# The fp4 layer of a perceiver kernel: the down product in three one-pass products, with GpSimd taking lower parts and the quantiser's last step

## The reference, cut to what matters

```
def fp4_quant_dequant(x):              # blocks of 16 along the last dimension
    scale = max(max(abs(block)) / 6, 1e-12)
    q = GRID[searchsorted(MID, abs(block / scale))] * sign(block) * scale
def fp4_linear(x, w):  return einsum('bsk,nk->bsn', fp4(x), fp4(w))
x = x + fp4_linear(silu(fp4_linear(ln(x), w_gate)) * fp4_linear(ln(x), w_up), w_down)   # 512 -> 1408 -> 512
```

## Time and profile before

| | |
|---|---|
| median of three runs | 1468.76 us |
| the profiled execution | 1466.26 us, span 1464.4 us, mean TensorE clock 0.981 |
| busy share of the span | TensorE 93%, VectorE 74%, ScalarE 40%, GpSimd 10% |
| the fp4 layer | from about 804 to 1057 us of the span |
| 1 MB loads of the next stage's keys | 7.0 us from issue to landing (page, part 6) |

### The profile page before, as it was taken

The page is one execution under the profiler, slowest core; times in us unless marked ns, Lnnn a source line. Parts: engine busy times, 40 slices in busy tenths (PEclk is TensorE's granted clock), DMA queues, the critical chain, the costliest instruction groups (busy, mean ns, idle before and its releaser), DMA issues. The chain is left out here.

```text
span 1464.4 us, 32483 instructions
## 1 busy us (share of the span) xinstructions
PE 1364.0 (93%) x13794; PEld 940.7 (64%) x13794; DVE 1083.9 (74%) x2221; ACT 587.7 (40%) x1234; POOL 149.3 (10%) x106
## 2 busy tenths in 40 slices
PE   9999999999999997999988889999799898888898
PEld 5677777777777775435565767667466555677443
DVE  5477777778778787773677699787577786765887
ACT  2344444444444433212223511111388885034543
POOL 3200000000000000230000000100000003154800
PEclk9999999999999999899989999999999999989999
DMA  7343344334443333400006000000355464000000
GB/s 263 105 138 100 119 126 130 113 120 142 152 162 125 113 93 119 149 1 1 3 3 240 28 1 1 0 1 1 119 203 229 178 208 158 35 3 2 8 23 29
DMA packets 50330, 136.88 MB, mean 93 GB/s; under 512 B 10974, under 2 KB 15838, under 8 KB 44043
## 3 DMA queue, kind: packets, MB, share of 16 engines
q1 hardware_dynamic: 50186, 134.82, 27.2%
HBM read 117.73 MB, written 17.07 MB: 92 GB/s over the span
## 5 line engine op out<-in xcount | busy, mean ns | idle before, releaser
L735 ACT ACTIVATE l0x_prob<-l0x_prob,l0x_negmax 128x512 f32<-128x512 f32 x128 | 90.9, 712 | 177.5 <-DVE l0x_negmax L802 177.5
L593 PE MATMUL bank<-l0x_ctxT,l0x_upper_k 128*128 128x512 f32 x256 | 106.8, 417 | 1.3 <-PEq L271 1.3
L606 PE MATMUL bank<-l0x_upper_v,l0x_ctxT 128*128 128x512 f32 x256 | 104.7, 409 | 0.0
L608 PE MATMUL bank<-l0x_upper_v,l0x_ctxT_lower 128*128 128x512 f32 x256 | 101.0, 394 | 0.0
L595 PE MATMUL bank<-l0x_ctxT,l0x_lower_k 128*128 128x512 f32 x256 | 100.8, 394 | 0.0
L607 PE MATMUL bank<-l0x_lower_v,l0x_ctxT 128*128 128x512 f32 x256 | 100.7, 393 | 0.0
L594 PE MATMUL bank<-l0x_ctxT_lower,l0x_upper_k 128*128 128x512 f32 x256 | 100.5, 392 | 0.0
L1071 PE MATMUL bank<-ident,l1x_prob 128*128 128x128 f32 x512 | 78.9, 288 | 13.2 <-ACT l1x_prob L1141 9.2
L1141 ACT ACTIVATE l1x_prob<-l1x_prob,l1x_negmax 128x512 f32<-128x512 f32 x128 | 91.0, 715 | 0.0
L1190 DVE CUSTOM_DVE_ANT_0 l1x_prob<-bank,l1x_zeros 128x512 f32<-128x512 f32 x128 | 80.8, 687 | 13.8 <-PE bank L1056 13.8
L1071 PEld LDWEIGHTS bank<-ident,l1x_prob 128*128 128x128 f32 x512 | 55.6, 143 | 51.0 <-ACT l1x_prob L1141 41.2
(11 more groups left out here) (346 smaller groups left out, 3125.6 us busy)
## 6 DMA issues: line engine op xcount, KB each, us to landing
l0x_whole<-in_turned_context SPq DMA_DIRECT2D x16, 1024.0 KB, 5.4
l1x_KT<-in_turned_context SPq DMA_DIRECT2D x16, 1024.0 KB, 7.0
l1x_ctx<-in_ctx SPq DMA_DIRECT2D x16, 1024.0 KB, 4.8
fp_weight<-l0x_weight_piece SPq DMA_DIRECT2D x24, 352.0 KB, 4.8
f_raw<-fp_weight SPq DMA_DIRECT2D x3, 2816.0 KB, 18.6
l0x_abs_piece<-in_L_ffn_w_gate SPq DMA_DIRECT2D x16, 512.0 KB, 4.4
l0x_abs_piece<-in_L_ffn_w_up SPq DMA_DIRECT2D x16, 512.0 KB, 5.4
l0x_abs_piece<-in_L_ffn_w_down SPq DMA_DIRECT2D x16, 512.0 KB, 4.5
```

Source lines behind the costliest of these rows:

```text
L593: nc.tensor.matmul(bank[:, :], w.upper_k[:, kc, cols], c, start=kc == 0, stop=False)
L606: nc.tensor.matmul(bank[:, :], c, w.upper_v[:, kc, :], start=kc == 0, stop=False)
L608: last = nc.tensor.matmul(bank[:, :], c_lower, w.upper_v[:, kc, :], start=False, stop=kc == CH - 1)
L735: nc.scalar.activation(w.prob[r][:, :], w.prob[r][:, :], ACT.Exp, scale=-1.0, bias=w.negmax[:, p:p + 1], accum_out=w.rowsum[:, b % 2, p:p ...
```

## The change

The down product is made of three one-pass products too. Upper parts of the down weights and of the turned hidden values are ScalarE copies; the lower parts, and those of the tokens, are GpSimd subtractions, from whole copies in SBUF. GpSimd also does step 9 of the quantiser for the hidden pieces (`hq_done`); VectorE does steps 0 to 8 (`HQ` = 9) and, since the scratch is shared, waits ahead of step 4 until GpSimd has read it. There are three sets of scale tensors. The first keys load moves to the layer's end. The head's normalised rows go to `w.head`, as `XN` now holds upper down weights; other addresses of the next stage's buffers move.

```diff
 @block.sync
-            loads(sp)
             sp.wait_ge(gate_up_full, TILES * R)
             late_loads(sp)                       # now keys 0, context 0, keys 1, context 1
 @block.gpsimd
+            def lower_tokens(t):
+                pool.wait_ge(x_upper, t + 1)
+                nc.gpsimd.tensor_tensor(w.x_lower[t % 2][:, :, :], w.x_whole[t % 2][:, :, :], w.x_upper[t % 2][:, :, :].bitcast(F32),
+                                        ALU.subtract).then_inc(x_lower, 1)
+            def last_step(t, r):
+                at, n = N0[r]
+                pool.wait_ge(step, (t * R + r + 1) * HQ)
+                if r == 0 and t > 0:
+                    pool.wait_ge(turn_full, t * R)
+                quantisers[(t * R + r) % 2].last(nc.gpsimd, w.hq[:, at:at + n], n).then_inc(hq_done, 1)
+            def lower_down(k):                   # DOWN_PARTS = ((0, 4), (4, 8), (8, IC0))
+                pool.wait_ge(down_upper, k + 1)
+                nc.gpsimd.tensor_tensor(w.down_lower[:, lo:hi, :], w.downT[:, lo:hi, :], down_part(lo, hi).bitcast(F32),
+                                        ALU.subtract).then_inc(down_lower, 1)
+            def lower_hidden(t):
+                for r, (at, n) in enumerate(N0):
+                    pool.wait_ge(h_upper, t * R + r + 1)
+                    nc.gpsimd.tensor_tensor(w.h_lower[:, at:at + n], w.hT[:, at:at + n], hidden_part(at, n).bitcast(F32),
+                                            ALU.subtract).then_inc(h_lower, 1)
+            lower_tokens(0)
+            lower_tokens(1)
+            pool.wait_ge(rstd_done, 1)
+            next_tokens(2)
+            for r in range(R):
+                last_step(0, r)
+                lower_down(r)
+            for t in range(LAST):
+                last_step(t + 1, 0)
+                lower_hidden(t)
+                if t + 2 < TILES:
+                    lower_tokens(t + 2)
+                last_step(t + 1, 1)
+                if t + 3 < TILES:
+                    next_tokens(t + 3)
+                last_step(t + 1, 2)
+            lower_hidden(LAST)
 @block.tensor, turn_hidden(t) and out_product(t)
-                pe.wait_ge(step, (t + 1) * (R * Q_STEPS))
+                pe.wait_ge(hq_done, (t + 1) * R)
-                for kc in range(IC0):
-                    ins = nc.tensor.matmul(work[1][:, :], w.hT[:, kc * P:(kc + 1) * P], w.downT[:, kc, :],
+            def upper_products(bank, lo, hi):
+                for kc in range(lo, hi):
+                    nc.tensor.matmul(bank[:, :], hidden_chunk(kc), down_chunk(kc), start=kc == 0, stop=False)
+                    nc.tensor.matmul(bank[:, :], hidden_chunk(kc), w.down_lower[:, kc, :], start=False, stop=False)
+            def out_product(t):
+                if t == 0:
+                    pe.wait_ge(down_lower, len(DOWN_PARTS))
+                pe.wait_ge(h_upper, t * R + R)
+                upper_products(work[1], 0, IC0)
+                pe.wait_ge(h_lower, t * R + R)
+                lower_products(work[1], 0, IC0).then_inc(out_full, 1)      # 11 of h_lower x down_chunk
 last_tile: per piece wait hq_done, transposes, wait h_upper, upper_products; then wait h_lower, lower_products
 @block.scalar, upper_tokens(t); upper_hidden(t, r) after the three hidden_copy(t, r); upper_down(k) after silu(0, r)
-                nc.scalar.activation(w.x_upper[t % 2][:, :, :], work[0][:, :]..., ACT.Copy).then_inc(x_upper, 1)
+                nc.scalar.activation(w.x_whole[t % 2][:, :, :], work[0][:, :]..., ACT.Copy).then_inc(x_whole, 1)
+                act.wait_ge(x_whole, t + 1)
+                nc.scalar.activation(w.x_upper[t % 2][:, :, :], w.x_whole[t % 2][:, :, :], ACT.Copy).then_inc(x_upper, 1)
 @block.vector, hidden(t); lower_tokens(t) is gone; tokens(t) keeps ten steps and waits for hq_done ahead of step 4
-                    for q in range(Q_STEPS):
+                    for q in range(HQ):
+                        if piece + q > 0:
+                            dve.wait_ge(step, piece * HQ + q)
+                        if q == 4 and piece > 0:
+                            dve.wait_ge(hq_done, piece)
```

More of the change, by code:

```diff
@@ L153, in __call__, with last @@
             return v.scalar_tensor_tensor(xn, pow2, -HALF_STEP, xn, ALU.mult, ALU.add)
-        return v.tensor_tensor(blocks(out), blocks(xn), wide(scale), ALU.mult)
+        return self.last(v, out, n)
+    def last(self, engine, out, n):
+        k, t = n // BLOCK, self.tmp
+        blocks = lambda ap: ap.rearrange("p (k e) -> p k e", e=BLOCK)
+        return engine.tensor_tensor(blocks(out), blocks(t.xn[:, 0:n]), t.scale[:, 0:k].unsqueeze(2).to_broadcast([P, k, BLOCK]),
+                                    ALU.mult)
 Q_STEPS = 10
@@ L2013, with fp4_layer @@
 HEAD_TILES = TILES - 1
-def fp4_layer(nc, g, w, loads, late_loads):
+def fp4_layer(nc, g, w, late_loads):
     s = lambda n: g.sems.take(f"ffn0_{n}")
@@ L2181, in last_tile @@
                     ins.then_inc(turn_full, 1)
[L2182 to L2186, removed]
+                    pe.wait_ge(h_upper, LAST * R + r + 1)
+                    upper_products(LAST_OUT, at // P, (at + n) // P)
+                pe.wait_ge(h_lower, LAST * R + R)
+                lower_products(LAST_OUT, 0, IC0).then_inc(out_full, 1)
                 pe.wait_ge(x_done, LAST)
@@ L2236, in silu, with hidden_copy, upper_hidden @@
                 nc.scalar.activation(w.silu[:, at:at + n], gate[r][:, 0:n], ACT.Silu).then_inc(silu_done, 1)
[L2238 to L2245, removed]
+            def hidden_copy(t, r):
+                at, n = N0[r]
+                act.wait_ge(turn_full, t * R + r + 1)
+                if r == 0 and t > 0:
+                    act.wait_ge(out_full, t)
+                bank = gate[r] if t == LAST else work[r % 2]
+                nc.scalar.activation(w.hT[:, at:at + n], bank[:, 0:n], ACT.Copy).then_inc(turned, 1)
+            def upper_hidden(t, r):
+                at, n = N0[r]
+                act.wait_ge(turned, t * R + r + 1)
+                nc.scalar.activation(hidden_part(at, n), w.hT[:, at:at + n], ACT.Copy).then_inc(h_upper, 1)
             upper_tokens(0)
@@ L2262, in _ @@
                 silu(0, r)
+            for k in range(len(DOWN_PARTS)):
+                upper_down(k)
             for t in range(LAST):
@@ L2369, in _ @@
             tokens(1)
-            lower_tokens(1)
             hidden(0)
@@ L3197, in fp4_buffers @@
         w.downT = a.over("f0_downT", wide, F32, "tm_kT")
+        w.down_lower = a.over("f0_down_lower", wide, F32R, "tm_kT")
+        w.down_upper = [a.over("f0_down_upper0", [P, TILES, D], F32R, "XN"),
+                        a.over("f0_down_upper1", [P, IC0 - TILES, D], F32R, "tm_XX", DOWN_REST_AT)]
+        w.h_upper = [a.over("f0_h_upper0", [P, 8 * P], F32R, "tm_XX", HIDDEN_UPPER_AT),
+                     a.over("f0_h_upper1", [P, INTER0 - 8 * P], F32R, "tm_XX", HIDDEN_REST_AT)]
+        w.h_lower = a.over("f0_h_lower", [P, INTER0], F32R, "tm_kT", size + 3 * INTER0 * 4)
+        w.head = a.over("f0_head", [P, HEAD_TILES, D], F32, "tm_mixed0", 2 * CH * TOK * 4 - size)
         w.silu, w.h, w.hq, w.hT = (a.over(f"f0_{n}", [P, INTER0], F32, "tm_kT", size + i * INTER0 * 4)
```

109 lines of the change are left out of this document (61 added, 48 removed).

## The result

The changed kernel took 1477.01 us (median of five runs, 1474.23 to 1478.64) beside 1467.66 us for the kernel before on the same chip: ratio 1.0065, 95% interval 1.0052 to 1.0078. A second set gave 1475.44 us beside 1467.77, ratio 1.0048 (1.0031 to 1.0064). It is slower, as forecast (1474.0, range 1464 to 1481). One of the nine executions of the experiment "wait by piece" took 2608 us at a granted clock of 0.941; its ratio leaves that one out, and without it the median is 1471.7.

What follows compares the result with a forecast made beforehand. TensorE was taken to bound each steady tile, with VectorE late in the first. Startup +11.0, steady tiles -5.3 and last tile -0.4 sum to +5.3 us: 1471.6 for the profiled execution, median 1474.0, range 1464 to 1481.

Steps and rivals of the forecast that it cites:

- The mechanism of the first tile: First tile: VectorE and GpSimd instructions with two SBUF inputs each wait for the other's whole instruction; startup +11.0 us.
- the walk: First tile followed step by step through the engines: first down product ends at 883.4 against 874.1, 9.3 us later.
- the clock term: First tile: after three TensorE idles of 4 us or more, products run longer at a lower clock; 1.7 us.
- Steady tiles: Tiles between startup and the last: down product 9.4 to 7.55 us, net 0.9 us saved each, six tiles 5.3 us.
- The wait term: Steady tile: down product waits for ScalarE's upper copies, ready 1.0 us after TensorE has turned the tokens.
- the sixth steady tile: Six tiles were counted as one kind, each saving 0.9 us, together 5.3 us.
- The last tile: Tile of 13.4 us: three added waits of 0.6, 0.6, 0.45 and a shorter down product; -0.4 us (0 to -0.6).
- The overlap that I granted: Last tile: waits overlapping the transposes bring its 13.2 us to between 12.8 and 13.2.
- that rival: Steady tile: GpSimd's lower parts come late by more than the 1 us margin; +11 and 1480 us; chance 0.08.
- the 2 to 4 forecast: Steady tile: VectorE gains waits for GpSimd of at most 2 to 4 us, staying under 26.6.
- VectorE as the bound: Every tile: VectorE stopped by GpSimd's two-input work, 29.7 against 27.5 us; total about 1493; chance 0.06.
- Partly stopped: First tile: engines stop each other part of the time, startup +3 to +8, sum -2.9 to +2.9; chance 0.21.

Runs made afterwards that it cites:

- wait by piece: Against the changed kernel, the down product's upper products wait for the upper copies of the hidden values piece by piece; 1472.54 us, ratio to before 1.0021.
- GpSimd alone: Against the changed kernel, the down product is float32 as before, while GpSimd keeps the last steps and token lower parts; 1467.91 us, ratio to before 0.9999.
- split down: Against the changed kernel, GpSimd's down-weight subtractions are eleven 512 wide instead of three 2048 or 1536 wide; 1478.39 us, ratio to before 1.0070.
- down from bank: Against the changed kernel, ScalarE takes the down weights' upper parts and VectorE their lower parts straight from the banks; 1475.30 us, ratio to before 1.0039.
- loads and places: The kernel before with only the later first keys load and the next stage's new addresses; 1470.61 us, then 1467.57 us in a second set.

## Why the prediction was right, and where it was not

**The mechanism of the first tile held.** Forecast for the walk: transposes 862.9, tokens 870.0, lower parts 880.9, end 883.4. Measured: 864.2, 871.5, 881.2, 883.9. The first product ends 10.2 us later from the layer's start than before (10.4 in the second profiles), and tile 1's transposes start 10.0 us later; the forecast was +11.0. Three things in it were wrong. I put the end of the old product at 874.1, while the gate product behind it starts at 873.7, so the walk's 9.3 us should have been 9.7. The stopped steps were 1 and 3, tensor_scalar of 32 or 24 numbers per partition, not step 4: VectorE was stopped 0.25 to 0.54 us after GpSimd began, where I had let it run on to the next two-input step. So up to 0.6 us more was left to do when it was released, part of the 1.3 us by which the transposes were later than forecast. And the clock term of 1.7 us was no cost: the granted clock did fall (0.76 between 856.0 and 883.9), the first ten upper products ran 0.43 us apart, but the lower products then waited 1.55 us for h_lower anyway. The term stood in the sum beside a wait that covered it.

**Steady tiles: -0.61 us each, not -0.9.** The wait term was right: the down product starts 0.95 us later within its tile (forecast 1.0). Its own length was 7.65 for 7.55. What I had not seen is the rest: from the product's end to the next transposes, 15.4 us instead of 15.2. The gate and up products of 512 columns, which the change doesn't touch, are 0.233 us apart on average, before 0.229 (means over some 90 starts between 930 and 985 us). In all fourteen profiles the spacing follows the form of the down product: 0.229 where it is float32, GpSimd alone included, and 0.233 where it is one-pass. Why it does is open.

**Tile 6 was counted as the sixth steady tile, and is none.** It turns no tokens, so the wait of 2.12 us lies bare. Forecast -0.9, measured +1.08. That the token transposes hid part of the wait stood in my own text (1.0 us after they are done); I applied it to a tile that has none. But the wait is the smaller part of the miss. In "split down" and "down from bank" tile 6 has the same wait and full clock behind it:

```profile
1042.30 0.47 PE L2224 MATMUL bank<-f_down_upper,f_h_upper 128*128 128x512 f32 x1 [2.12 <-ACT f_h_upper L2328]
1042.61 0.40 PE L2225 MATMUL bank<-f_down_lower,f_h_upper 128*128 128x512 f32 x1
1042.85 0.40 PE L2224 MATMUL bank<-f_down_upper,f_h_upper 128*128 128x512 f32 x1
```

There it takes 11.74 us, 0.2 less than before. So of the 2.0 us by which the forecast was off, 0.7 are the bare wait and 1.3 the low clock behind it (0.57 between 1037 and 1041 us in the changed kernel), a term that the prediction had in the first tile alone. In the sum: five tiles give -3.0, tile 6 +1.1, together -2.0 for the -5.3 forecast.

**The last tile**: 13.40 to 13.52 us, +0.1 for -0.4. The waits grew from 0.69, 0.69 and 0.58 to 1.35, 1.35 and 1.13, +1.87 for the +1.65 of the sum. The overlap that I granted did not come.

**GpSimd's lower parts** came 1.8 us ahead of their use in the steady tile (933.29 against 935.13; forecast 1.0), so that rival had nothing. **VectorE** is busy 24.2 us in a tile of 26.9 where it was busy 22.6 in 27.5. It gave away 2.5 us of steps, so it loses some 4 us a tile to GpSimd, the upper end of the 2 to 4 forecast, without becoming the bound: behind the first tile every wait of TensorE over 0.3 us, up to the next stage, is for ScalarE.

**Two sums of the rivals** don't come out of their own terms. VectorE as the bound was priced at 21.9 + 7.8 = 29.7 us a tile, but 22.6 less the 2.5 that it sheds is 20.1, which gives 27.9 and a total near 1482, not 1493. "Partly stopped" gives -2.7 to +2.3 us and not -2.9 to +2.9. Neither moves the forecast.

**The sum.** Layer: +10.0 (up to tile 1's transposes) -3.0 (five tiles) +1.1 (tile 6) +0.1 (last) = +8.2, forecast +5.3. The two errors, 1.0 too much at startup and 3.9 too little behind it, partly cancel: the total lies well in the range in part by luck. The medians say +7.7 to +9.4, so the layer alone is enough to explain them. The profiled executions show another 2.1 to 4.3 us behind the layer. Part is at its entry: the second group of key products takes 2.01 us in the changed kernel

```profile
1071.59 2.01 PE L1055 MATMUL bank<-l1x_KT,XNT 32*64 32x512 f32 x16
1073.53 1.68 PE L1070 MATMUL bank<-ident,l1x_prob 128*128 128x128 f32 x8
```

where the kernel before took 1.73 us there, and 0.9 us is lost within 9 us of the stage. All profiles in which GpSimd does the last steps have it (0.6 to 1.2 us), those of "loads and places" do not (1.82 and 1.74 us for that group). The rest differs between executions of one kernel as much as between kernels. Whether it is owed to the change is open.

## What to carry to other kernels

A GpSimd subtraction with two inputs in SBUF is paid by VectorE, one whole instruction at a time, and it costs the kernel where VectorE is the late engine: here 12.7 us of it cost 10.8 us of the first tile. Splitting it gave back about 1 us. What helped was to take it out of that stretch, to ScalarE or to VectorE's own idle time: find that gap in VectorE's timeline first, here 10 us ahead of the first hidden piece. The short last steps cost the first tile nothing. Where a product waits for several copies, let each part wait for the copy that it reads: three lines gave 5.1 us of layer (6.4 with the low clock of tile 6), where the one-pass product itself had brought 3.0 in five tiles. Walk the tile that lacks the covering step (here the second to last) by itself. And a new wait of TensorE can have a second price, which a walk has to hold: of the ten waits of 2.1 to 4.0 us inside a down product's work in these profiles, eight had slow products behind them, which took 1.3 to 1.6 us longer, and two had not.

## What was not expected of the hardware

- An instruction of 0.18 us and 32 numbers per partition with one SBUF input stood 4.40 us beside a GpSimd subtraction (846.78); a RECIPROCAL (0.30, 856.17) beside such a subtraction and a TENSOR_REDUCE (0.55, 855.37) beside GpSimd's last step did not stand at all.
- GpSimd's own operations differ. Its TENSOR_SCALAR of 2.07 us let VectorE's step 4 pass at 0.69, in this and in the four other tiles of the kernel before where the two meet, while its TENSOR_TENSOR of 1.3 us and its copy of 0.75 us don't. The Trainium skill (SBUF — State Buffer, Who interferes with whom) makes no such difference; here the measurement decides. It does not let all pass: VectorE's next step in the kernel before, a tensor_scalar, took 0.78 us for 0.43.

```profile
864.45 0.78 DVE L147 TENSOR_SCALAR f_qpow<-f_qxn 128x512 int32<-128x512 int32 x1
```

- Gate and up products of 512 columns are 0.233 us apart in a tile whose down product is one-pass too, and 0.229 where it is float32, at a granted clock of 1.00 in both.
- A wait of 0.79 us behind the transposes is followed, in some tiles of some executions and not in others, by eight products at 0.43 us: 1.6 us a time. That may be why "down from bank" spreads over 14 us; only its profiled execution has a trace, so it is not shown. "Wait by piece", without that wait, had no such products behind the first tile in its profile.
- The 11 first lower products took 2.65 to 2.67 us behind waits of 1.29, 1.47, 1.55 and 1.64 us, and 4.16 to 4.22 us behind waits of 2.56, 2.69 and 4.02 us.
